# One message-passing layer of a graph network: rows of B loaded once for two blocks of edges, from ScalarE's queue, and the edges laid out with four blocks in a partition

## The reference

```
h   = relu(concat(x[src], x[dst]) @ Wm1 + bm1)       # 256 wide
h   = relu(h @ Wm2 + bm2)
msg = h @ Wm3 + bm3                                  # 128 wide
agg = segment_sum(msg, dst) / max(count(dst), 1)
upd = relu(concat(x, agg) @ Wn1 + bn1) @ Wn2 + bn2
out = layernorm(x + (x + upd))
```

## Time and profile before

| What | Value |
|---|---|
| time, median of 3 runs | 1202.34 us (1200.86 to 1204.38) |
| the profiled execution's own span | 1416.6 us |
| TensorE busy (PE) | 1249.7 us, 88% |
| VectorE busy (DVE) | 979.6 us, 69% |
| ScalarE busy (ACT) | 740.6 us, 52% |
| GpSimd busy (POOL) | 786.5 us, 56% |
| granted TensorE clock, mean | 0.993 |
| moved by DMA | 211.42 MB, 149 GB/s |
| b_win<-b_table, issued by SP | 391 DMAs of 128 KB |
| rel<-rel_dram, issued by SP | 196 DMAs of 128 KB |

### The profile page before, as it was taken

The page is one execution under the profiler, slowest core; times in us unless marked ns, Lnnn a source line. Parts: engine busy times, 40 slices in busy tenths (PEclk is TensorE's granted clock), DMA queues, the critical chain, the costliest instruction groups (busy, mean ns, idle before and its releaser), DMA issues.

```text
span 1416.6 us, 33766 instructions
## 1 busy us (share of the span) xinstructions
PE 1249.7 (88%) x9614; PEld 1172.0 (83%) x9615; DVE 979.6 (69%) x2072; ACT 740.6 (52%) x1392; POOL 786.5 (56%) x814
## 2 busy tenths in 40 slices
PE   6978888888888888888888889988999989899997
PEld 6868888888888888888888888888888888888886
DVE  6846666766766666766766766767767767777676
ACT  3544555555555555555555555555554555545585
POOL 2166666666666666666666666666666666564000
PEclk9999999999999999999999999999999999999999
DMA  9665555545545555555545555455545454554022
GB/s 308 274 234 156 146 144 151 149 141 151 151 140 150 152 142 147 151 143 147 152 139 150 146 143 151 145 144 152 139 147 151 138 150 144 145 151 142 10 67 86
DMA packets 135605, 211.42 MB, mean 149 GB/s; under 512 B 24247, under 2 KB 102669, under 8 KB 134030
## 3 DMA queue, kind: packets, MB, share of 16 engines
q1 hardware_dynamic: 98030, 108.43, 25.3%
q0 software_dynamic: 37536, 102.55, 25.1%
HBM read 188.09 MB, written 22.80 MB: 149 GB/s over the span
## 4 chain that ended last, share of the span: by engine, by line
PE 80%; issue 12%; DVE 2%; SPq 1%; another core or an unknown queue 1%; DMA 1%; ACT 1%; DVEq 1%; ACTq 0%
PE bank L1437 39%; PE bank L1413 11%; PE bank L1324 6%; PE sums L1345 4%; PE sums L1341 4%; PE sums L1347 3%; PE sums L1349 3%; PE bank L1478 2%; PE sums L1491 1%; PE bank L1234 1%; PE bank L1219 1%; PE bank L1461 1%; PE sums L1219 1%; DMA b_win<-b_table 1%
## 5 line engine op out<-in xcount | busy, mean ns | idle before, releaser
L630 POOL DMA_INDIRECT a_edge<-a_table,src_idx x782 | 767.1, 981 | 457.8 <-remote 268.2
L1437 PE MATMUL bank<-w,h 128*128 128x256 f32 x4692 | 661.4, 283 | 104.9 <-issue 102.1
L1437 PEld LDWEIGHTS bank<-w,h 128*128 128x128 f32 x4692 | 596.5, 188 | 119.7 <-issue 118.7
L1106 DVE SCALAR_TENSOR_TENSOR h<-bank,h 128x512 fp32r<-128x512 f32 x391 | 268.7, 687 | 338.4 <-issue 326.7
L732 ACT ACTIVATE h<-bank 128x512 fp32r<-128x512 f32 x391 | 233.8, 598 | 475.3 <-remote 439.2
L721 ACT COPY bank<-b_bc 128x512 f32<-128x512 f32 x391 | 231.5, 592 | 115.2 <-issue 66.7
L1118 DVE SCALAR_TENSOR_TENSOR h_lo<-bank,h_hi 128x512 fp32r<-128x512 f32 x391 | 266.5, 681 | 0.1
L1413 PE MATMUL bank<-ident,a_edge 128*128 128x128 f32 x1564 | 237.4, 274 | 21.1 <-issue 16.6
L740 ACT ACTIVATE h_hi<-bank 128x512 fp32r<-128x512 f32 x391 | 232.6, 595 | 2.8 <-PE bank L1437 2.8
L1413 PEld LDWEIGHTS bank<-ident,a_edge 128*128 128x128 f32 x1564 | 180.3, 140 | 40.5 <-issue 34.2
L1324 PE MATMUL bank<-onehot_t,b_win 128*128 128x256 f32 x782 | 190.3, 325 | 0.0
(11 more groups left out here) (190 smaller groups left out, 682.7 us busy)
## 6 DMA issues: line engine op xcount, KB each, us to landing
b_win<-b_table SPq DMA_DIRECT2D x391, 128.0 KB
rel<-rel_dram SPq DMA_DIRECT2D x196, 128.0 KB
a_edge<-a_table,src_idx POOLq DMA_INDIRECT x782
a_table<-work SPq DMA_DIRECT2D x12, 512.0 KB, 4.6
b_table<-work SPq DMA_DIRECT2D x5, 1024.0 KB
b_table<-h SPq DMA_DIRECT2D x4, 1024.0 KB
f_x<-in_x SPq DMA_DIRECT2D x12, 256.0 KB, 5.2
b_table<-a_edge SPq DMA_DIRECT2D x3, 1024.0 KB, 5.8
```

The source lines that it names most:

```text
L630: pool.indirect_dma_start(a_edge[:, b % R * TB + t, :], None, a_table, bass.IndirectOffsetOnAxis(ap=src_idx[:, b * TB + t:b * TB + t + 1], ...
L1106: dve.scalar_tensor_tensor(h1[:, k % U, 1, :], bank[k % 2][:, :], 0.0, h1[:, k % U, 0, :].bitcast(F32), ALU.max, ALU.subtract).then_inc(s_ ...
L1437: ins = pe.matmul(to, h1[:, j, a, h * EB + t * P:h * EB + (t + 1) * P], w2[:, b, h, :], start=False, stop=(a == 1 and h == KH - 1), skip_g ...
```

## The change

The edges are laid out anew: partition p holds the four blocks 4p to 4p+3 one after the other, 1024 numbers. Two loads for each of dst and src take the place of five: 97 rows of 1024 numbers, and one row of 672. The stores of minima and maxima and of the relative positions become one each. The positions of a block now count from the lowest node of its pair of blocks (pair_low), and so do the far words. b_win holds one window of 64 nodes for a pair. SP loads the first two; the later ones are issued by ScalarE, for the next body, after the relu of each odd block.

```diff
-        loads = []
-        for n in range(2):
-            for g in range(GR):
-                rows = min(full - g * BG, BG)
-                if rows:
-                    loads.append((n, g, 0, rows, EB))
-            if E % EB:
-                loads.append((n, GR - 1, rows, 1, E % EB))
+        RUN = GR * EB
+        rows, rest = E // RUN, E % RUN
+        loads = [(n, row, many, edges) for n in range(2) for row, many, edges in ((0, rows, RUN), (rows, 1, rest))]
...
-            for n, g, row, rows, edges in loads:
-                at, e0 = (n * GR + g) * EB, (g * BG + row) * EB
-                sp.dma_start(edges_in[row:row + rows, at:at + edges],
-                             (dst, src)[n][e0:e0 + rows * edges].rearrange("(b e) -> b e", e=edges)
+            for n, row, many, edges in loads:
+                at, e0 = n * RUN, row * RUN
+                sp.dma_start(edges_in[row:row + many, at:at + edges],
+                             (dst, src)[n][e0:e0 + many * edges].rearrange("(b e) -> b e", e=edges)
                              ).then_inc(s_edges, 16)
...
-                    for j in range(GR):
-                        sp.dma_start(mm_dram[j * BG:(j + 1) * BG, :], minmax_i[0:BG, 2 * j:2 * j + 2]
-                                     ).then_inc(s_scr, 16)
+                    sp.dma_start(mm_dram.rearrange("(p g) c -> p (g c)", g=GR), minmax_i[0:BG, :]
+                                 ).then_inc(s_scr, 16)
...
-                    for j in range(GR):
-                        sp.dma_start(rel_dram[j * BG:(j + 1) * BG, :],
-                                     rel16[0:BG, j * EB:(j + 1) * EB]).then_inc(s_scr_rel, 16)
+                    sp.dma_start(rel_dram.rearrange("(p g) e -> p (g e)", g=GR), rel16[0:BG, :]
+                                 ).then_inc(s_scr_rel, 16)
...
+            first = load_words(sp, words_sp, 0, NP, PAD_DST)
+            for c in range(NP):
+                sp.dma_start(b_win[:, c, :].bitcast(F32), b_table[bass.ds(first[c] * 2, P), :]
+                             ).then_inc(s_bw[c], 16)
             def body(i):
-                first = load_words(sp, words_sp, i * U, U, PAD_DST)
-                for k in range(U):
-                    if there(i, k - RB):
-                        sp.wait_ge(s_ex, i * U + (k - RB + (2 if k % 2 == 0 else 1)))
-                    if k % 2 == 0:
-                        sp.dma_start(rel[:, k // 2, :].rearrange("p (b e) -> p b e", b=2),
-                                     rel_dram[bass.ds(i * U + k, 2), :].partition_broadcast(P)
-                                     ).then_inc(s_rc[k // 2], 16)
-                    if there(i, k):
-                        sp.dma_start(b_win[:, k % RB, :].bitcast(F32),
-                                     b_table[bass.ds(first[k] * 2, P), :]).then_inc(s_bw[k % RB], 16)
+                for c in range(NP):
+                    if there(i, 2 * c - U):
+                        sp.wait_ge(s_ex, i * U + (2 * c - U + 2))
+                    sp.dma_start(rel[:, c, :].rearrange("p (b e) -> p b e", b=2),
+                                 rel_dram[bass.ds(i * U + 2 * c, 2), :].partition_broadcast(P)
+                                 ).then_inc(s_rc[c], 16)
...
 (ScalarE, body)
+                last = isinstance(i, int) and i == NI - 1
+                first = [] if last else load_words(act, words_sp, i * NP + NP, NP, PAD_DST)
...
                         act.activation(h1[:, k % U, 0, :], bank[k % 2][:, :], ACT.Relu).then_inc(s_h1h, 1)
+                        if k % 2 and not last:
+                            act.dma_start(b_win[:, k // 2, :].bitcast(F32), b_table[bass.ds(first[k // 2] * 2, P), :]
+                                          ).then_inc(s_bw[k // 2], 16)
...
 (VectorE)
+                dve.tensor_tensor(pair_low[0:BG, :], minmax[0:BG, 0:2 * GR:4], minmax[0:BG, 2:2 * GR:4], ALU.min
+                                  ).then_inc(s_wi, 1)
-                dve.tensor_tensor(rel16[0:BG, :].rearrange("p (g e) -> p g e", g=GR), dst_f,
-                                  minmax[0:BG, 0:2 * GR:2].unsqueeze(2).to_broadcast([BG, GR, EB]), ALU.subtract
+                dve.tensor_tensor(rel16[0:BG, :].rearrange("p (c e) -> p c e", c=NP),
+                                  edges_f[0:BG, 0:GR, :].rearrange("p (c g) e -> p c (g e)", c=NP),
+                                  pair_low[0:BG, :].unsqueeze(2).to_broadcast([BG, NP, 2 * EB]), ALU.subtract
                                   ).then_inc(s_rel16, 1)
...
-                dve.tensor_copy(words_sp[0:1, :], lowest).then_inc(s_rw, 1)
-                dve.tensor_tensor(far, highest, lowest, ALU.subtract).then_inc(s_rw, 1)
+                dve.tensor_tensor(words_sp[0:1, :], row_in[0:1, 0:2 * NB:4], row_in[0:1, 2:2 * NB:4], ALU.min
+                                  ).then_inc(s_rw, 1)
+                dve.wait_ge(s_rw, 2)
+                dve.tensor_tensor(by_pairs(far), by_pairs(highest), pair_lowest, ALU.subtract).then_inc(s_rw, 1)
...
-                dve.wait_ge(s_bw[k % RB], nth(i, k, 16))
+                    dve.wait_ge(s_bw[k // 2 % RC], nth(i, k, 16))
```

More of the change, by code:

```diff
@@ L22 @@
 RC = 2
+NP = U // 2
 AHEAD = 2
@@ L79, in gnn_layer @@
         dst_col = sb("dst_col", [P, NB * TB], F32)
-        words_sp = sb("words_sp", [1, NB], I32)
+        words_sp = sb("words_sp", [1, NB // 2], I32)
         words_act = sb("words_act", [1, NB + 2 * U], I32)
@@ L187, in gnn_layer @@
         first_start = carve(GR)
+        pair_low = carve(GR // 2)
         dst_place = carve(GR, EB).bitcast(I32)
@@ L261, in gnn_layer @@
         s_rc = [sem(f"s_rel_loaded{c}") for c in range(RC)]
-        s_bw = [sem(f"s_b_win_loaded{c}") for c in range(RB)]
+        s_bw = [sem(f"s_b_win_loaded{c}") for c in range(RC)]
         s_bf = sem("s_b_far_loaded")
@@ L443, in gnn_layer @@
         assert NW * P // QUARTER <= 256
-        full = E // EB
-        assert (GR - 1) * BG <= full
-        loads = []
-        for n in range(2):
-            for g in range(GR):
-                rows = min(full - g * BG, BG)
-                if rows:
-                    loads.append((n, g, 0, rows, EB))
-            if E % EB:
-                loads.append((n, GR - 1, rows, 1, E % EB))
+        RUN = GR * EB
+        rows, rest = E // RUN, E % RUN
+        assert BG - 1 <= rows + (rest > 0) <= BG and GR == U and rest
+        loads = [(n, row, many, edges) for n in range(2) for row, many, edges in ((0, rows, RUN), (rows, 1, rest))]
         NPAIR = pair(NG - 1, (size(NG - 1) + 1) // 2 - 1)
@@ L577, in _ @@
                                base=0, pattern=[[-1, P]], channel_multiplier=1).then_inc(s_const, 1)
-            pool.memset(edges_in[:, (GR - 1) * EB:GR * EB], PAD_DST).then_inc(s_pad, 1)
-            pool.memset(edges_in[:, (2 * GR - 1) * EB:2 * GR * EB], 0).then_inc(s_pad, 1)
+            pool.memset(edges_in[:, rest:RUN], PAD_DST).then_inc(s_pad, 1)
+            pool.memset(edges_in[:, RUN + rest:2 * RUN], 0).then_inc(s_pad, 1)
             pool.memset(f_x[:, NW - 1, :], 0.0).then_inc(s_xz, 1)
@@ L614, in _ @@
             pool.wait_ge(s_et, 2 * GR)
-            pool.wait_ge(s_scr_rel, 16 * GR)
+            pool.wait_ge(s_scr_rel, 16)
             pool.wait_ge(s_bz, 16)
@@ L645, in edge_columns @@
                     act.wait_ge(s_et, n * GR + g // 2 * 2 + 2)
-                    act.copy(col[:, g * BG * TB:(g + 1) * BG * TB].rearrange("p (b t) -> p t b", t=TB),
+                    act.copy(col[:, :].rearrange("p (b g t) -> p g t b", g=GR, t=TB)[:, g, :, :],
                              bank[6 + g // 2][:, g % 2 * TB * BG:(g % 2 + 1) * TB * BG]
@@ L886, in _, with by_pairs @@
             far = row_far[0:1, 0:NB]
+            pair_lowest = words_sp[0:1, :].unsqueeze(2).to_broadcast([1, NB // 2, 2])
+            def by_pairs(row):
+                return row.rearrange("p (c k) -> p c k", k=2)
             def ranges_and_spans():
@@ L902, in first_words @@
                 dve.wait_ge(s_rw, 6)
-                dve.scalar_tensor_tensor(words_act[0:1, 0:NB], far, float(2**13), lowest, ALU.mult, ALU.add
-                                         ).then_inc(s_rw, 1)
+                dve.scalar_tensor_tensor(by_pairs(words_act[0:1, 0:NB]), by_pairs(far), float(2**13), pair_lowest,
+                                         ALU.mult, ALU.add).then_inc(s_rw, 1)
                 dve.tensor_scalar(row_start[0:1, :], row_third[0:1, :], float(STRIDE // QUARTER), None, ALU.mult
@@ L1383, in expand_and_sum @@
                             expand_far(k)
-                    expand(b_win[:, k % RB, :], onehot_t[:, k % 2, :], k).then_inc(s_ex, 1)
+                    expand(b_win[:, k // 2 % RC, :], onehot_t[:, k % 2, :], k).then_inc(s_ex, 1)
                 if there(i, k - BACK):
```

6 lines of the change are left out of this document (3 added, 3 removed).

## The result

The changed kernel takes 1242.18 us, median of 4 runs (1239.77 to 1244.86); the kernel before took 1202.9 us beside it (1200.86 to 1204.38). The ratio is 1.0326, 95% interval 1.0311 to 1.0341: 39.3 us slower, where 36.8 were predicted. About 27 us come from two loads of edges that run on one DMA engine each, about 9 us from three blocks near the end that need far rows of B, and the rest for the most part from the new layout. The profiled execution spans 1239.0 us at a mean granted clock of 0.981.

What follows compares the result with a forecast made beforehand. TensorE's 2.57 us steps were taken to bound the blocks, SP's serial load issue to limit the lead-in. Terms 27 + 0.8 + 9 = 36.8 us took 1202.34 to 1239 us; range 1228 to 1256, with rival 1 1208 to 1256.

Steps and rivals of the forecast that it cites:

- Base: Whole kernel before: lead-in of 89 us, 390 dense TensorE steps of 2.57 us, tail of 109 us.
- Edges, 27 us: Lead-in: both 97-row edge loads share one DMA engine, ending at 38.5 us instead of 11.48; 27 us later (24.5 to 38).
- its signs: Lead-in: cast waits until 36 to 45 us; DMA share about 0.06 to 0.1 between about 15 and 36 us.
- Words and stores, nothing: Fewer stores, pair_low and a minimum replacing a copy: costed at nothing (-1 to +0.5 us).
- rival 1: Lead-in: edges spread over most engines; SP's saving removes VectorE's 2.18 us wait, far spans remain; 1210 us, chance 0.12.
- First loads of B, +0.8 us: Before the first one-hot: two b_win loads go ahead of rel, issued about 0.9 us later; +0.8 us (0 to 1.2).
- B for a pair, nothing: Edge blocks: half the b_win loads go, ScalarE issues the rest within its spare time; nothing (-5 to +5 us).
- rivals 3 and 4: Edge blocks: 3, B's rows came late before, now sooner, 1190 us, chance 0.05; 4, ScalarE's load too late, 1297 us, 0.04.
- Far spans, 9 us: Blocks 383, 387 and 389 near the end need far loads: 3 us each, 9 in all (0.7 to 12.4).
- Rivals 1 and 2: Lead-in edge loads: 1, spread over most engines, 1210 us, chance 0.12; 2, one engine each, different ones, 1224 us, 0.13.
- The range: Whole kernel: 1228 (24.5 us, far spans at 2) to 1256 us (38 us, far spans at 4).
- its 0.91 for slower: Whole kernel: chance of slower, from the forecast, rivals 1, 2, 4 and most of the rest; no change 0.04, faster 0.05.

Runs made afterwards that it cites:

- (1): The 96-row cut: the changed kernel with each 97-row edge load cut into 96 rows and one row; 1215.09 us, ratio 1.0105.
- (6): The kernel before, B by block from SP, with the new edge layout alone, its single stores and 96-row loads; 1204.74 us, ratio 1.0016.
- (11): Against (6): edge columns kept by quarter, so ScalarE's copies write every second number again; 1203.54 us, ratio 1.0008.
- (5): Against (1): the pair's window of B issued by SP behind the pair's rel instead of by ScalarE; 1213.99 us.
- 9: Against (1): VectorE makes a far block's second one-hot right after the block's first, not at the end of its step; 1212.85 us.
- 10: Against 9: ScalarE also issues a far block's rows of B one block earlier; 1210.95 us, ratio 1.007.

## Why the prediction was right

*Base.* Lead-in 89, dense steps of 2.57, tail 109: the second profile of the kernel before has its first transposes at 89.84, steps of 2.57 us and a span of 1201.2 us. Reading the steps before pricing anything was what kept the 214 us out of the sum.

*Edges, 27 us.* Measured 27.1 us in the runs, 28.53 us at the cast. One engine, 26 to 27 GB/s, end at 40 us against the 38.5 taken. That nothing covers it held (1). What the prediction did not see is that the loads hold SP itself, for 15.80 us: the later loads were not behind the edges on that engine, they were not yet issued. So the share of 0.06 lasts only until SP is free at 24.50, not until 36 as its signs say, and then the loads of x run beside the second load of edges. Up to the copies this cost nothing more, 34.59 us from the cast against 34.47. The prediction also moved the lead-in as one piece, to 117 us for the first transposes, and they stand at 120.45: with the 28.53 at the cast, 2.4 us came in behind it, most of it at the strided copies and by the clock behind them, a part of the layout that the prediction did not price at all. This term is missing from its sum. In the runs the layout without one-engine loads costs 2.2 us (6), near the 2.5 us by which the sum fell short; about half of that went with the copies (11).

*Words and stores, nothing.* Right in size. The side remark that six issues less would bring A's store forward by 2.4 us was wrong (6), so rival 1's -2.2 us was no gain to be had: the 96-row cut is rival 1's kernel and takes 1215, not 1210.

*First loads of B, +0.8 us.* VectorE waits 3.27 us for rel instead of 2.95, so 0.3; too small for the runs to tell.

*B for a pair, nothing.* Right, and rivals 3 and 4 are out: TensorE's 3423 matmuls in 400 us are the same, and neither queue matters to what the runs can tell (5). The ground given was weak, though: "VectorE waited for b_win twice" is a reading of the one execution with the long steps. In the second profile VectorE waits 109 times; what hides the waits is that TensorE has work all the time.

*Far spans, 9 us.* 9.35 us in the runs. The mechanism was half of it: the load's way to its landing and VectorE's one-hot, which stands at the end of its step, are late together (by the medians 9 took away 2.2 us, 10 a further 1.9), and the clock can fall behind the stall. The prediction had only the load, and it took TensorE to stand 2 to 4 us where it stood 1.5 to 1.9; that the total came out at 9 all the same is in part luck. (The reference's draw gives at most 35 nodes for a block, not 44; either is well under 64.)

*Rivals 1 and 2.* Rival 1 is out by the cast at 40.01, rival 2 by the share of 0.06: both loads shared one engine.

*The range.* With the terms that it names its ends come to 1229.6 and 1253 us rather than 1228 and 1256, and its 0.91 for slower is the forecast with rivals 1, 2 and 4 alone. Neither touches the outcome.

## What to carry to other kernels

Count the rows of a DMA's slowest dimension before anything else: here 97 rows, a prime count, put a load on one engine and 94 on two, and one row more than 96 cost 27 us on top of 1215. When a change makes a window cover more, count from the data how often the slow path is taken and what TensorE waits for there; three of 391 blocks cost 9 us. And where a profile's span is 18% over the runs, find the steps that are longer before summing against it.

## What the runs showed that was not expected

- A load on one DMA engine holds the queue that issued it: 15.80 us for two issues (1.92 us for five before); with 94 rows on two engines, 6.27 us for three.
- Six issues fewer on SP did not bring the loads behind them forward: the two broadcasts behind the loads of x took 3.24 to 3.51 us to issue in nine kernels, where they had taken 1.13 and 1.28.
- Four copies of 128x196 on ScalarE took 1.57 us when they wrote every eighth number of a row, and 1.02 us when they wrote every second.
- The same stall of TensorE, 1.85 and 1.87 us, left the granted clock at 1.00 in one profile and at 0.55 to 0.62 in another; so did a stall of 2.14 and 2.15 us in the lead-in, with 0.50 to 0.67 and 1.00.
- Of two profiled executions of one kernel, one spanned 1416.6 us and the other 1201.2.
